# First attention: the key tiles that take a relative bias, moved to other places in the order of the scores

## The chip, the core and the metric

The program runs on one core of a Trainium2 chip. The metric is the device time of one execution in microseconds (us), as the median of several. TensorE is called PE here, VectorE DVE, ScalarE ACT, GpSimd POOL, and SP is the queue that issues most DMAs.

## What is computed

The input is 4096 tokens of 256 numbers. A first attention with 16 heads of 16 numbers, over all 4096 tokens, has a bias that depends on the clipped distance of query and key:

```
scores = jnp.einsum('bhid,bhjd->bhij', qh, kh)
rel = jnp.clip(pos[None, :] - pos[:, None], -K, K) + K          # K = 64
bias_r = jnp.einsum('bhid,rd->bhir', qh, rel_pe)
bias = jnp.take_along_axis(bias_r, jnp.broadcast_to(rel[None, None], (b, h, l, l)), axis=-1)
attn = jax.nn.softmax(scores + bias, axis=-1)
out = jnp.einsum('bhij,bhjd->bhid', attn, vh)
```

A layernorm and two layers of windowed attention and feed-forward follow. The change is in the first attention alone, which takes the span from about 250 to 3755 us.

## The kernel before

`attend` works through 128 chunks: 16 heads, each with 8 chunks of 512 queries. For a chunk all 32 tiles of 128 keys are scored. The keys are laid out so that tile 0 is the first of the chunk's own four tiles; tile 31 is the one just before them. Where query and key are more than 64 apart the bias is one of two edge values, which are part of the key rows, so the score matmul brings it along. Tiles 0, 1 and 2 need one edge on one side and the other on the other side: two matmuls (`score`, L516 and L519). Near the diagonal something has to be added: to tiles 0 to 4 and to tile 31, in all six additions of DVE (`near_add`, L741) from `near_bias` onto the scores in PSUM, 192, 256, 256, 192, 64 and 64 columns wide.

Scores come in **pairs** of tiles, 16 to a chunk (`PAIRS`). Pair s lies in the PSUM buffer `scores[s % 2]`; ACT makes its exponentials in one instruction (`exp_pair`, L642) into `probs`. `score` of pair s waits until the exponential of pair s - 2 is done. Where a pair takes additions, its exponential also waits for `near_added`.

Before a chunk can be scored its row maxima must be known. They come from 32 **max groups** (`max_group`, L490, with additions to the near ones by matmul, L494): each is one 512-wide matmul into one of three shared PSUM banks, which DVE reads with a reduce (`bank_max`, L765) before the bank is used again. These groups run 16 slots ahead of the chunk. The three banks are handed on in a fixed order (`SHARED_USES`), in which the two halves of a bias block (`make_bias`, L542, read by ACT in `keep_bias`, L633), the maxima turned to rows (L502) and the final sum of a chunk (L551) have places too: the bank of the first bias half is that of max group in slot 1, the next max groups take the banks after groups 2 and 3.

The order is written out by hand. A chunk has eight **turns** on PE; in each turn come the value matmuls of two pairs (`pv_quad`, L531), then four **slots**, each with one max group, and two pairs of scores behind the first and the second slot:

```
for turn in range(QUADS):
    pv_quad(n, par, turn)
    for i in range(4):
        slot = 4 * turn + i
        max_slot(n, par, bias, slot, ahead)
        for c in SLOT_SCORES[i]:        # ((0, 1), (2, 3), (), ())
            if turn < QUADS - 2:
                score(n, par, 4 * (turn + 2) + c)
            elif ahead:
                score(n + 1, 1 - par, 4 * (turn - QUADS + 2) + c)
```

So turns 0 to 5 score pairs 4 to 15 of the chunk, turns 6 and 7 pairs 0 to 3 of the next one. Turns 0 and 1 also hold the two halves of a bias block, in all chunks but the last nine. After turn 7 comes `sum_quadrants`, four transposes of `out_copy`, which ACT copies behind the exponential of pair 1.

DVE goes slot by slot: the read of the slot's max group, `near_add` ahead of some of them (`NEAR_SLOTS`), and at the end of the chunk `finish` (L773, L775, L777: out_sum, inv_sum, tokens). SP loads the keys for two chunks ahead in four pieces, each when a given pair has been scored (`PIECES`, third number). Chunks run two to a pass of a hardware loop on each engine.

Of the kernel before, what the change touches and what calls it, by code (L numbers as in the profile page):

```python
# [22 lines left out]
P = 128  # L23
# [3 lines left out]
TILES = N // P  # L27
# [7 lines left out]
CH = 512  # L35
CHUNKS = N // CH
TPC = CH // P
# [8 lines left out]
VW = D + 1  # L46
WIN_TILES = TILES + TPC - 1
SLAB = 2 * P
PAD = CLIP
PAIRS = TILES // 2  # L50
# [183 lines left out]
def attend(nc, q_parts, k_parts, v_wide, rel_T, ident, attn):  # L234
# [9 lines left out]
    LEAD = 16  # L244
    TOTAL = HEADS * CHUNKS
    SLOT_SCORES = ((0, 1), (2, 3), (), ())
    NEAR_SLOTS = (26, 27, 30, 23)
    ROWS_SLOT = 20
    MAX_GROUPS = TPC * (TILES // TPC)
    with ExitStack() as ctx:  # L250
# [3 lines left out]
        keys = [sb(f"keys{i}", [ROWS + MROWS, WIN_TILES * P], BF16) for i in range(2)]  # L254
        queries = [sb(f"queries{i}", [ROWS + MROWS, CH], BF16) for i in range(2)]
        max_queries = [sb(f"max_queries{i}", [ROWS, CH], BF16) for i in range(2)]
        values = [sb(f"values{i}", [P, TILES, VW]) for i in range(2)]
# [26 lines left out]
        out_ps = ps("out_ps", [P, CH])  # L284
# [11 lines left out]
        table_ready = sem("table_ready")  # L296
        cleared = sem("cleared")
        ident_ready = sem("ident_ready")
        PIECES = ((0, 8, 3), (8, 16, 7), (16, 24, 11), (24, WIN_TILES, 15))
        keys_in = [[sem(f"keys_in{i}_{j}") for j in range(4)] for i in range(2)]  # L300
        queries_in = [sem(f"queries_in{i}") for i in range(2)]
        max_queries_in = [sem(f"max_queries_in{i}") for i in range(2)]
# [13 lines left out]
        near_added = sem("near_added")  # L316
# [9 lines left out]
        def place(n):  # L326

            return n // CHUNKS, n % CHUNKS

        @block.sync  # L330
        def _(sp):
# [3 lines left out]
            def load_keys(n, par, j):  # L335
                h, c = place(n)
                a, b, _ = PIECES[j]
                row = 0
# [39 lines left out]
            with sp.Fori(0, TOTAL // 2 - 1) as m:  # L378
                for par in range(2):
# [3 lines left out]
                    for j in range(4):  # L383
                        sp.wait_ge(scores_ready, n * PAIRS + PIECES[j][2] + 1)
                        load_keys(n + 2, par, j)
# [74 lines left out]
        def _(pe):  # L460
# [45 lines left out]
            def score(n, par, c):  # L506

                s = c // 2
                if c == 0:
                    pe.wait_ge(queries_in[par], (n // 2) * QUERY_DMAS + QUERY_DMAS)  # L510
                    pe.wait_ge(max_placed, n + 1)
                if c % 2 == 0:
                    pe.wait_ge(exp_done, n * PAIRS + s + 1)
                cut = min(c + 1, TPC) * P
                out = scores[s % 2][:, c % 2, :]
                mm = pe.matmul(out[:, 0:cut], keys[par][:, c * P:(c + 1) * P],  # L516
                               queries[par][:, 0:cut], start=True, stop=True)
                if cut < CH:
                    mm = pe.matmul(out[:, cut:CH], keys[par][:, (c + TILES) * P:(c + TILES + 1) * P],  # L519
                                   queries[par][:, cut:CH], start=True, stop=True)  # L520
                if c % 2 == 1:
                    mm.then_inc(scores_ready, 1)

            def pv_quad(n, par, q):

                if q == 0:
                    pe.wait_ge(values_in[par], (n // 2) * 16 + 16)
                    pe.wait_ge(out_copied, n + 1)
                pe.wait_ge(exp_done, n * PAIRS + 2 * q + 4)
                for i in range(4):  # L530
                    mm = pe.matmul(out_ps[32 * i:32 * i + VW, :], values[par][:, 4 * q + i, :],  # L531
                                   probs[(2 * q + i // 2) % 4][:, i % 2, :],
                                   start=q == 0, stop=q == QUADS - 1, skip_group_check=True)
                mm.then_inc(pv_done, 1)
# [74 lines left out]
            for c in range(8):  # L609
                score(0, 0, c)  # L610
# [12 lines left out]
        @block.scalar  # L623
        def _(act):
            act.preload_act_table(ACT.Exp)
            act.sem_inc(exp_done, 2)
            for semaphore in (out_copied, normed, out_summed, max_rows):
                act.sem_inc(semaphore, 1)

            def keep_bias(block_no, half):  # L630
                h, b = place(block_no)
                act.wait_ge(bias_ready, block_no * 2 + half + 1)
                act.activation(near_bias[:, bass.ds(h % 2, 1), 1:TILES + 1, bass.ds(b * BLOCK_U + half * UG, UG)],  # L633
                               shared("bias", half).rearrange("p (a u j) -> p a j u", a=1, u=UG), ACT.Copy
                               ).then_inc(bias_read, 1)

            def exp_pair(n, s):
                if s in (0, 1, 2, PAIRS - 1):
                    act.wait_ge(near_added, n * 4 + {0: 1, 1: 2, 2: 3, PAIRS - 1: 4}[s])
                act.wait_ge(scores_ready, n * PAIRS + s + 1)  # L640
                act.wait_ge(pv_done, n * QUADS + s // 2 + 1)
                act.activation(probs[s % 4][:], scores[s % 2][:], ACT.Exp).then_inc(exp_done, 1)  # L642

            def place_max(n, par):
                act.wait_ge(max_rows, n + 2)
                act.activation(queries[par][ROWS:ROWS + MROWS, :], shared("rows", 0)[ROWS:ROWS + MROWS, :], ACT.Copy
                               ).then_inc(max_placed, 1)

            def chunk(n, par, bias, more):

                for s in range(4, PAIRS):
                    if s == PAIRS - 2 and more:
                        place_max(n + 1, 1 - par)
                    exp_pair(n, s)
                    if bias and s in (5, 7):
                        if s == 5:
                            act.wait_ge(window_ready, n + 1)
                        keep_bias(n + NEXT_GEN, s // 7)
                for s in range(4):
                    if more:  # L660
                        exp_pair(n + 1, s)
                    if s == 1:
                        act.wait_ge(pv_done, n * QUADS + QUADS + 2)
                        act.wait_ge(out_summed, n + 1)
                        act.activation(out_copy[:], out_ps[:], ACT.Copy).then_inc(out_copied, 1)

            act.wait_ge(cleared, 10)
            for e in range(NEXT_GEN):
                for half in range(2):
                    keep_bias(e, half)  # L670
            place_max(0, 0)
            for s in range(4):
                exp_pair(0, s)
            last_bias = (TOTAL - NEXT_GEN) // 2
            with act.Fori(0, last_bias) as m:
                for par in range(2):
                    chunk(m * 2 + par, par, True, True)
            chunk(2 * last_bias, 0, True, True)
            chunk(2 * last_bias + 1, 1, False, True)
            with act.Fori(last_bias + 1, TOTAL // 2 - 1) as m:  # L680
                for par in range(2):
                    chunk(m * 2 + par, par, False, True)
            chunk(TOTAL - 2, 0, False, True)
            chunk(TOTAL - 1, 1, False, False)

        @block.vector
        def _(dve):
# [43 lines left out]
            def near_add(n, s):  # L731
                h, c = place(n)

                spans = {0: [(0, 0, 192, 1, 64), (1, 64, 320, 2, 0)],
                         1: [(0, 192, 448, 3, 0), (1, 320, 512, 4, 0)],
                         2: [(0, 448, 512, 5, 0)],
                         PAIRS - 1: [(1, 0, 64, 0, 192)]}[s]
                dve.wait_ge(scores_ready, n * PAIRS + s + 1)
                for tile, a, b, slab, u in spans:
                    part = scores[s % 2][:, tile, a:b]  # L740
                    ins = dve.tensor_tensor(part, part,  # L741
                                            near_bias[:, bass.ds(h % 2, 1), bass.ds(c * TPC + slab, 1), u:u + b - a],
                                            ALU.add)
                ins.then_inc(near_added, 1)
# [35 lines left out]
            def chunk(n, par, ahead):  # L780
                for slot in range(MAX_GROUPS):
                    k = LEAD + slot
                    if slot == NEAR_SLOTS[3]:
                        near_add(n, PAIRS - 1)
                    if ahead and slot in NEAR_SLOTS[:3]:
                        near_add(n + 1, NEAR_SLOTS.index(slot))
                    if k < MAX_GROUPS and ahead >= 1:
                        bank_max(n + 1, 1 - par, k, shared("max", slot))
                    if k >= MAX_GROUPS and ahead >= 2:
                        bank_max(n + 2, par, k - MAX_GROUPS, shared("max", slot))  # L790
                    if ahead >= 1 and MAX_GROUPS - 1 <= k <= MAX_GROUPS + 1:
                        (find_max, cut_high, cut_low)[k - MAX_GROUPS + 1](n + 1, 1 - par)
                finish(n)
# [5 lines left out]
            cut_low(0, 0)  # L799
            for k in range(LEAD):  # L800
                bank_max(1, 1, k, shared_ps[(MAX_GROUPS + k) % 3][:])
            for s in range(3):
                near_add(0, s)
            with dve.Fori(0, TOTAL // 2 - 1) as m:
                for par in range(2):
# [1031 lines left out]
```

## Time and profile before

| | |
|---|---|
| median of 3 runs | 5559.55 us (5557.49 to 5559.81) |
| profiled execution | 5559.1 us, its span 5557.4 us |
| PE busy | 5118.3 us (92%) |
| DVE busy | 4185.6 us (75%) |
| ACT busy | 3111.0 us (56%) |
| max-group reads, L765 | 4096 of 686 ns |
| exponentials, L642 | 2048 of 1021 ns |
| additions, L741 | 768 of 334 ns on average |

The shares are averages over the whole program; the stage of the change has its own. Matmuls overlap in the records, so the gap between two starts says more than a duration, and the same holds for DVE: one instruction's record begins before the one ahead has ended.

### The profile page before, as it was taken

The numbers are of one execution on the slowest core, as the hardware profiler recorded it, in microseconds if no ns is written. First come the engines' busy times: TensorE is split into PE (matmuls) and PEld (weight loads), VectorE is DVE, ScalarE is ACT, GpSimd is POOL, SyncE is SP. The second block draws the span as 40 slices with busy tenths as digits, with TensorE's granted clock in tenths as the row PEclk, the third lists the DMA queues.
The fourth block names the chain that finished last, engine by engine and source line by source line (L and its number), as shares of the span: only waits on it lengthen the run. The fifth ranks groups of instructions, "written<-read, shape, count | busy, mean of one in ns | idle before, by whom it ended". The sixth has DMA issues, their size and how long they took to land. (4 is left out here: it accounts for less than half of the span.)

```text
span 5557.4 us, 114988 instructions
## 1 busy us (share of the span) xinstructions
PE 5118.3 (92%) x33760; PEld 2655.6 (48%) x33760; DVE 4185.6 (75%) x8817; ACT 3111.0 (56%) x4539; POOL 997.1 (18%) x791
## 2 busy tenths in 40 slices
PE   7599999999999999999999999998599989899989
PEld 4233333333333333333333333334488867788866
DVE  6488888888888888888888888871477744677755
ACT  4266666666666666666666666670266532456521
POOL 0211111111111111111111111100233310233211
PEclk9599999999999999999999999995699999999999
DMA  6312212212122122121221211211200000000010
GB/s 203 76 49 55 54 48 54 52 52 54 49 55 54 48 54 54 49 54 48 54 54 48 55 48 48 52 40 33 95 1 0 0 17 0 17 0 0 1 38 23
DMA packets 199610, 248.32 MB, mean 45 GB/s; under 512 B 60575, under 2 KB 128485, under 8 KB 197733
## 3 DMA queue, kind: packets, MB, share of 16 engines
q1 hardware_dynamic: 194388, 226.76, 14.9%
q0 software_dynamic: 5136, 20.45, 1.9%
q8 instruction: 50, 0.82, 0.1%
q14 instruction: 36, 0.29, 0.0%
HBM read 210.72 MB, written 36.18 MB: 44 GB/s over the span
## 5 line engine op out<-in xcount | busy, mean ns | idle before, releaser
L765 DVE TENSOR_REDUCE group_max<-shared_ps 128x1 f32<-128x512 f32 x4096 | 2668.6, 686 | 536.6 <-PE shared_ps L490 430.6
L642 ACT ACTIVATE probs<-scores 128x1024 f32<-128x1024 f32 x2048 | 2012.0, 1021 | 995.7 <-PE scores L516 619.4
L490 PE MATMUL shared_ps<-keys,max_queries 96*128 96x512 bf16 x4096 | 1444.0, 385 | 10.8 <-issue 1.7
L516 PE MATMUL scores<-queries,keys 98*128 98x512 bf16 (+3 forms) x4096 | 1212.8, 370 | 92.6 <-ACT probs L642 91.5
L531 PE MATMUL out_ps<-probs,values 128*17 128x512 f32 x8192 | 1079.1, 599 | 0.4 <-ACT probs L642 0.4
L490 PEld LDWEIGHTS shared_ps<-keys,max_queries 96*128 96x128 bf16 x4096 | 395.2, 96 | 1149.2 <-DVE group_max L765 544.2
L231 POOL TENSOR_TENSOR near_window<-near_bias,one_f 128x1536 bf16<-128x1536 f32 x128 | 351.4, 2746 | 2909.1 <-DVE max_parts L759 2263.7
L516 PEld LDWEIGHTS scores<-queries,keys 98*128 98x128 bf16 x4096 | 359.0, 98 | 466.2 <-ACT probs L642 242.8
L542 PE MATMUL shared_ps<-block_q,block_table 96*128 96x32 bf16 x4096 | 271.6, 233 | 107.6 <-POOL block_q L427 80.7
L542 PEld LDWEIGHTS shared_ps<-block_q,block_table 96*128 96x128 bf16 x4096 | 231.3, 114 | 197.9 <-issue 148.6
L1191 POOL TENSOR_TENSOR norm<-norm,layer_expo 128x16 f32<-128x16 f32 x64 | 186.2, 2910 | 705.4 <-DVE norm L1577 705.4
L1449 ACT ACTIVATE sim_prob<-sim_prob,shift,norm 128x256 f32<-128x256 f32 x512 | 299.5, 588 | 10.0 <-DVE shift L1647 10.0
L531 PEld LDWEIGHTS out_ps<-probs,values 128*17 128x17 f32 x8192 | 136.1, 95 | 264.7 <-issue 191.4
L494 PE MATMUL shared_ps<-ident_b,near_window 128*128 128x128 bf16 x1536 | 255.4, 220 | 0.0
L633 ACT ACTIVATE near_bias<-shared_ps 128x512 f32 (+1 forms) x256 | 152.8, 597 | 179.5 <-PE shared_ps L542 179.4
L741 DVE TENSOR_TENSOR scores<-scores,near_bias 128x192 f32<-128x192 f32 (+2 forms) x768 | 234.2, 334 | 20.7 <-PE scores L516 16.5
L1297 PEld LDWEIGHTS bank<-v_kept,prob_T 128*128 128x128 f32 x2048 | 238.2, 192 | 7.5 <-issue 2.0
L1297 PE MATMUL bank<-v_kept,prob_T 128*128 128x64 f32 x2048 | 235.8, 274 | 1.2 <-DVE tokens L1609 1.2
L1429 ACT ACTIVATE squares<-bank 128x512 f32<-128x512 f32 x128 | 76.5, 598 | 262.5 <-PE bank L1250 262.5
L494 PEld LDWEIGHTS shared_ps<-ident_b,near_window 128*128 128x128 bf16 x1536 | 151.3, 99 | 123.3 <-issue 2.2
L1504 ACT ACTIVATE gate<-quad,b 128x512 f32<-128x512 f32 x96 | 66.1, 688 | 236.9 <-PE quad L1371 236.9
L1642 DVE CUSTOM_DVE_ANT_0 sim_prob<-quad,mask 128x256 f32<-128x256 f32 x512 | 181.9, 420 | 16.5 <-issue 13.3
(195 smaller groups left out, 5777.3 us busy)
## 6 DMA issues: line engine op xcount, KB each, us to landing
keys<-k_parts SPq DMA_DIRECT2D x384, 96.0 KB, 2.1
values<-v_wide SPq DMA_DIRECT2D x128, 272.0 KB, 2.7
keys<-k_parts SPq DMA_DIRECT2D x384, 64.0 KB, 2.0
keys<-k_parts SPq DMA_DIRECT2D x128, 132.0 KB, 2.4
k_parts<-part SPq DMA_DIRECT2D x96, 128.0 KB
queries<-q_parts SPq DMA_DIRECT2D x768, 16.0 KB, 1.7
max_queries<-q_parts SPq DMA_DIRECT2D x768, 16.0 KB, 1.7
keys<-k_parts SPq DMA_DIRECT2D x384, 32.0 KB, 1.9
```

Of the source, the lines that this page charges most:

```text
L231: return pool.tensor_tensor(out, in_, ones[:].to_broadcast(list(in_.shape)), ALU.mult)
L490: mm = pe.matmul(bank, max_queries[par][:, t * P:(t + 1) * P], keys[par][0:ROWS, (t + TPC * g) * P:(t + TPC * (g + 1)) * P], start=True, s ...
L494: mm = pe.matmul(bank[:, pos * P:(pos + 1) * P], near_window[par][:, slab, u:u + P], ident_b[:], start=False, stop=i == len(near) - 1)
L516: mm = pe.matmul(out[:, 0:cut], keys[par][:, c * P:(c + 1) * P], queries[par][:, 0:cut], start=True, stop=True)
L531: mm = pe.matmul(out_ps[32 * i:32 * i + VW, :], values[par][:, 4 * q + i, :], probs[(2 * q + i // 2) % 4][:, i % 2, :], start=q == 0, stop ...
L542: mm = pe.matmul(shared("bias", half)[:, i * TILES:(i + 1) * TILES], block_table[par][:, BLOCK_U - 1 - u:BLOCK_U - 1 - u + P], block_q[par ...
L642: act.activation(probs[s % 4][:], scores[s % 2][:], ACT.Exp).then_inc(exp_done, 1)
L741: ins = dve.tensor_tensor(part, part, near_bias[:, bass.ds(h % 2, 1), bass.ds(c * TPC + slab, 1), u:u + b - a], ALU.add)
L765: dve.tensor_reduce(group_max[par][:, k:k + 1], bank, AX.X, ALU.max).then_inc(max_read, 1)
L1191: pool.tensor_tensor(norm[par][:], norm[par][:], expo[:, 0:2 * LHEADS].rearrange("p (h a) -> p h a", a=1), ALU.pow).then_inc(S.norm_ready, 1)
L1297: mm = pe.matmul(o_ps[:, j * LD:(j + 1) * LD], prob_T[:, 2 * j + c, :], v[:, h * LD:(h + 1) * LD], start=c == 0, stop=c == 1)
L1449: ins = act.activation(prob[:, h, :], sim[:, h, :], ACT.Exp, bias=shift[:, head:head + 1], scale=norm[par][:, head, :], accum_out=total[:, ...
```

## The change

The order of the key tiles becomes a table, `ORDER`: place c of a chunk's 32 scores holds tile `ORDER[c]`. The same table selects the values in `pv_quad`. Tiles with additions are now in pair 2 (tile 0), 3 (tile 1), 4 (tile 2), 5 (tiles 3 and 4) and 10 (tile 31); before they were in pair 0 (tiles 0 and 1), 1 (tiles 2 and 3), 2 (tile 4) and 15 (tile 31). DVE does them in front of other slots, and two key pieces are released by other pairs.

```diff
-    NEAR_SLOTS = (26, 27, 30, 23)
+    ORDER = (5, 6, 7, 8, 0, 9, 1, 10, 2, 11, 3, 4, 12, 13, 14, 15, 16, 17, 18, 19, 20, 31,
+             21, 22, 23, 24, 25, 26, 27, 28, 29, 30)
+    NEAR_SPANS = {2: [(0, 0, 192, 1, 64)], 3: [(0, 64, 320, 2, 0)], 4: [(0, 192, 448, 3, 0)],
+                  5: [(0, 320, 512, 4, 0), (1, 448, 512, 5, 0)], 10: [(1, 0, 64, 0, 192)]}
+    NEAR_PAIRS = tuple(NEAR_SPANS)
+    NEAR_SLOTS = {30: 2, 31: 3, 2: 4, 3: 5, 14: 10}
...
-        PIECES = ((0, 8, 3), (8, 16, 7), (16, 24, 11), (24, WIN_TILES, 15))
+        PIECES = ((0, 8, 5), (8, 16, 7), (16, 24, 12), (24, WIN_TILES, 15))
...
-                cut = min(c + 1, TPC) * P
+                tile = ORDER[c]
+                cut = min(tile + 1, TPC) * P
...
-                    mm = pe.matmul(out_ps[32 * i:32 * i + VW, :], values[par][:, 4 * q + i, :],
+                    mm = pe.matmul(out_ps[32 * i:32 * i + VW, :], values[par][:, ORDER[4 * q + i], :],
...
-                if s in (0, 1, 2, PAIRS - 1):
-                    act.wait_ge(near_added, n * 4 + {0: 1, 1: 2, 2: 3, PAIRS - 1: 4}[s])
+                if s in NEAR_PAIRS:
+                    act.wait_ge(near_added, n * len(NEAR_PAIRS) + NEAR_PAIRS.index(s) + 1)
...
-                spans = {0: [(0, 0, 192, 1, 64), (1, 64, 320, 2, 0)],
-                         1: [(0, 192, 448, 3, 0), (1, 320, 512, 4, 0)],
-                         2: [(0, 448, 512, 5, 0)],
-                         PAIRS - 1: [(1, 0, 64, 0, 192)]}[s]
...
-                    if slot == NEAR_SLOTS[3]:
-                        near_add(n, PAIRS - 1)
-                    if ahead and slot in NEAR_SLOTS[:3]:
-                        near_add(n + 1, NEAR_SLOTS.index(slot))
+                    if slot in NEAR_SLOTS:
+                        if NEAR_SLOTS[slot] >= 4:
+                            near_add(n, NEAR_SLOTS[slot])
+                        elif ahead:
+                            near_add(n + 1, NEAR_SLOTS[slot])
...
-            for s in range(3):
+            for s in NEAR_PAIRS[:2]:
                 near_add(0, s)
```

Lines behind the table stand eight or fewer lines later in the new file: the reads of max groups are L769 there, the additions L745.

DVE in turns 6 and 7, before (`group_max` is the read of one max group, slot 26 the first shown; rows that set registers are left out):

```order
L741 TENSOR_TENSOR scores0<-scores0,near_bias 128x192
L741 TENSOR_TENSOR scores0<-scores0,near_bias 128x256
L765 TENSOR_REDUCE group_max0<-shared_ps2 128x1
...
L741 TENSOR_TENSOR scores1<-scores1,near_bias 128x256
L741 TENSOR_TENSOR scores1<-scores1,near_bias 128x192
L765 TENSOR_REDUCE group_max0<-shared_ps0 128x1
...
L741 TENSOR_TENSOR scores0<-scores0,near_bias 128x64
...
L773 TENSOR_REDUCE out_sum<-shared_ps2 128x68
```

DVE from slot 29 in turn 7 to the end of the chunk, after:

```order
L769 TENSOR_REDUCE group_max0<-shared_ps2 128x1
...
L745 TENSOR_TENSOR scores0<-scores0,near_bias 128x192
...
L769 TENSOR_REDUCE group_max0<-shared_ps0 128x1
...
L745 TENSOR_TENSOR scores1<-scores1,near_bias 128x256
...
L769 TENSOR_REDUCE group_max0<-shared_ps1 128x1
L777 TENSOR_REDUCE out_sum<-shared_ps2 128x68
...
L781 TENSOR_TENSOR tokens<-out_sum,inv_sum 128x4x16
```

Pairs 0 and 1 had two additions each ahead of slots 26 and 27; now slots 28 and 29 are read first, and one addition each stands ahead of slots 30 and 31, just before the end of the chunk.

DVE in turn 0, from slot 1 to slot 3, after (before, the four reads of this turn stood there with nothing between them):

```order
L769 TENSOR_REDUCE group_max0<-shared_ps1 128x1
...
L745 TENSOR_TENSOR scores0<-scores0,near_bias 128x256
...
L769 TENSOR_REDUCE group_max0<-shared_ps2 128x1
...
L745 TENSOR_TENSOR scores1<-scores1,near_bias 128x192
...
L745 TENSOR_TENSOR scores1<-scores1,near_bias 128x64
...
L769 TENSOR_REDUCE group_max0<-shared_ps0 128x1
```

The additions on pairs 4 and 5 have moved between the reads of slots 1, 2 and 3.

## Rows read from the trace of the kernel before

**Rows 1.** Busy time in a stretch of the steady stage: PE, weight loads, DVE, ACT, POOL, granted clock, DMA share, GB/s.

```profile
1000.00:1600.00 600.00, 578.15 (x3992) 220.02 (x3991) 503.17 (x956) 392.30 (x437) 97.10 (x82) 1.00 0.21 52
```

**Rows 2.** Waits from 400 to 3400 us: us in total, times, longest.

```profile
PEld scores L516 <- ACT probs L642: 198.7, 327, 0.9
...
ACT probs L642 <- DVE scores L741: 314.5, 370, 1.7
```

**Rows 3.** Timeline of PE, a turn without waits: start, us, instruction.

```profile
2002.44 1.05 PE L531 MATMUL out_ps<-probs,values 128*17 128x512 f32 x8
...
2003.43 0.39 PE L490 MATMUL shared_ps<-keys,max_queries 96*128 96x512 bf16 x1
...
2003.65 0.60 PE L516 MATMUL scores<-queries,keys 98*128 98x512 bf16 x2
...
2005.27 1.05 PE L531 MATMUL out_ps<-probs,values 128*17 128x512 f32 x8
```

**Rows 4.** Timeline of PE, turns 6 to 1, second kind of chunk.

```profile
2016.31 0.38 PE L490 MATMUL shared_ps<-keys,max_queries 96*128 96x512 bf16 x1
2016.63 0.34 PE L516 MATMUL scores<-queries,keys 98*128 98x384 bf16 x1
...
2017.60 1.05 PE L531 MATMUL out_ps<-probs,values 128*17 128x512 f32 x8
2018.58 0.39 PE L490 MATMUL shared_ps<-keys,max_queries 96*128 96x512 bf16 x1
...
2019.33 0.61 PE L516 MATMUL scores<-queries,keys 98*128 98x512 bf16 x2 [0.35 <-ACT probs L642]
2019.77 0.38 PE L490 MATMUL shared_ps<-keys,max_queries 96*128 96x512 bf16 x1
2020.56 0.61 PE L516 MATMUL scores<-queries,keys 98*128 98x512 bf16 x2 [0.41 <-ACT probs L642]
...
2025.46 1.07 PE L542 MATMUL shared_ps<-block_q,block_table 96*128 96x32 bf16 x16 [0.28 <-DVE group_max L765]
```

**Rows 5.** Timeline of DVE: additions, reads, the end of two chunks (first and second kind).

```profile
1995.22 0.43 DVE L773 TENSOR_REDUCE out_sum<-shared_ps 128x68 f32<-128x272 f32 x1
...
1996.22 2.47 DVE L765 TENSOR_REDUCE group_max<-shared_ps 128x1 f32<-128x512 f32 x4
...
2015.16 0.22 DVE L741 TENSOR_TENSOR scores<-scores,near_bias 128x64 f32<-128x64 f32 x1
...
2017.34 0.71 DVE L741 TENSOR_TENSOR scores<-scores,near_bias 128x192 f32<-128x192 f32 x2
2017.96 0.68 DVE L765 TENSOR_REDUCE group_max<-shared_ps 128x1 f32<-128x512 f32 x1
2018.56 0.69 DVE L741 TENSOR_TENSOR scores<-scores,near_bias 128x256 f32<-128x256 f32 x2
...
2022.62 0.43 DVE L773 TENSOR_REDUCE out_sum<-shared_ps 128x68 f32<-128x272 f32 x1
...
2024.04 2.48 DVE L765 TENSOR_REDUCE group_max<-shared_ps 128x1 f32<-128x512 f32 x4 [0.33 <-PE shared_ps L490]
```

**Rows 6.** Timeline of ACT, the exponential of pair 0.

```profile
2018.25 1.02 ACT L642 ACTIVATE probs<-scores 128x1024 f32<-128x1024 f32 x1 [1.68 <-DVE scores L741]
```

**Rows 7.** Timeline of PE, turn 7 and the bias half, first kind.

```profile
1990.29 1.05 PE L531 MATMUL out_ps<-probs,values 128*17 128x512 f32 x8
...
1997.63 1.07 PE L542 MATMUL shared_ps<-block_q,block_table 96*128 96x32 bf16 x16 [0.17 <-DVE group_max L765]
```

**Rows 8.** Timeline of PE, end of chunk, two chunks apart: with a bias block, and without.

```profile
1994.03 0.60 PE L551 MATMUL shared_ps<-ident_f,out_copy 128*128 128x128 f32 x4
...
2049.16 0.60 PE L551 MATMUL shared_ps<-ident_f,out_copy 128*128 128x128 f32 x4
...
3613.05 0.60 PE L551 MATMUL shared_ps<-ident_f,out_copy 128*128 128x128 f32 x4
...
3663.53 0.60 PE L551 MATMUL shared_ps<-ident_f,out_copy 128*128 128x128 f32 x4
```

More of the change, by code:

```diff
@@ L513, in score @@
                     pe.wait_ge(exp_done, n * PAIRS + s + 1)
-                cut = min(c + 1, TPC) * P
+                tile = ORDER[c]
+                cut = min(tile + 1, TPC) * P
                 out = scores[s % 2][:, c % 2, :]
-                mm = pe.matmul(out[:, 0:cut], keys[par][:, c * P:(c + 1) * P],
+                mm = pe.matmul(out[:, 0:cut], keys[par][:, tile * P:(tile + 1) * P],
                                queries[par][:, 0:cut], start=True, stop=True)
                 if cut < CH:
-                    mm = pe.matmul(out[:, cut:CH], keys[par][:, (c + TILES) * P:(c + TILES + 1) * P],
+                    mm = pe.matmul(out[:, cut:CH], keys[par][:, (tile + TILES) * P:(tile + TILES + 1) * P],
                                    queries[par][:, cut:CH], start=True, stop=True)
@@ L732, in near_add @@
                 h, c = place(n)
-                spans = {0: [(0, 0, 192, 1, 64), (1, 64, 320, 2, 0)],
-                         1: [(0, 192, 448, 3, 0), (1, 320, 512, 4, 0)],
-                         2: [(0, 448, 512, 5, 0)],
-                         PAIRS - 1: [(1, 0, 64, 0, 192)]}[s]
                 dve.wait_ge(scores_ready, n * PAIRS + s + 1)
-                for tile, a, b, slab, u in spans:
+                for tile, a, b, slab, u in NEAR_SPANS[s]:
                     part = scores[s % 2][:, tile, a:b]
```

## Prediction, made before the change was run

> **What bounds the kernel now.** I read the stretches of the first attention first. In its steady stage PE is busy 578 of 600 us, DVE 503 and ACT 392, at a granted clock of 1.00 (2.4 GHz) [rows 1]; nothing in DMA comes near. So PE carries the time, and the question is where it stands still. The Trainium skill (Perfetto Trace Analysis, Identifying the Most-Contended Engine) says that matmul busy time is no measure of TensorE's headroom, since pipelined matmuls overlap in it. The trace agrees: a wait that the timeline books as 0.35 us idle is longer when it is measured from start to start (below).
>
> The list of waits over 3000 us, 109 chunks, comes next: ACT waited 314.5 us for DVE's additions to the scores, and the weight loads of the scores waited 198.7 us for ACT's exponentials [rows 2]. The chain is addition (DVE), exponential (ACT), next scores into the same buffer (PE).
>
> Then the timeline of one chunk. A turn without trouble starts its next turn 2.83 us later; its first max group starts 0.99 us after the value matmuls, the scores 0.22 us behind that group [rows 3]. In turn 6 and 7 it looks different [rows 4]: pair 1 starts 0.32 us behind its group instead of 0.22; pair 2 starts 0.75 us behind group 28 (0.53 lost), pair 3 0.79 us behind group 29 (0.57 lost). Pair 0 had been scored by about 2016.5, but its exponential started at 2018.25 after 1.68 us idle [rows 6], because DVE reaches its two additions only at 2017.34 [rows 5] and both stand in front of it. So 1.20 us per chunk go to the additions on pairs 15, 0 and 1.
>
> Who would be late next? After turn 7 PE goes through the sum and turn 0 to the first half of the bias block. Its bank is that of max group 1, which DVE must have read, behind the end of the chunk (out_sum, inv_sum, tokens). From the start of turn 7 to the bias matmuls it takes 7.34 us in one kind of chunk [rows 7] and 7.86 in the other [rows 4]. The two kinds alternate: DVE needs 1.00 us from out_sum to the next read, and 1.42 us where its loop turns round [rows 5]. Already here the bias matmuls start right as DVE ends its second read: in the second kind 2024.04 + 0.60 + 0.69 = 2025.33, bias at 2025.46. **The DVE chain is thus the limit of the stretch already, with the ACT waits in front of it.**
>
> **The change, part by part.** No matmul, read, addition or exponential is added or removed; the six additions keep their widths. A wait per chunk on ACT is added (five marked pairs, not four), one DVE wait on scores too, both on semaphores that are long up.
>
> *Pairs 0 and 1 lose their additions.* Their exponentials then start when scored: pair 0 in turn 6 from about 2016.5 to 2017.5, pair 1 to 2018.5; pairs 2 and 3 are wanted at 2018.8 and 2019.5. Both waits (0.53 and 0.57 us) go. Pair 15 loses its 64-wide addition (0.22 us [rows 5]), and with it the 0.10 us at pair 1 in turn 6.
>
> *What DVE does then in turn 7.* Measured from the value matmuls of turn 7. Group 28 starts at 0.99 and has landed at 1.4. From there DVE has four reads, 0.60 us from one to the next (2017.96 to 2018.56), and the additions on pairs 2 (192 wide) and 3 (256 wide). Those two widths together took 0.62 us in pair 0 (2017.34 to 2017.96) [rows 5]. With 0.05 us of waiting for group 29, out_sum starts at 1.4 + 2.40 + 0.62 + 0.05 = 4.5. Then 1.00 (1.42) us, the two reads of 0.60 + 0.69, and 0.12 us to PE: the bias block starts at **6.9 (7.3)** where it started at 7.34 (7.86). Gain 0.43 (0.53) us. The rest of the 1.10 us is given back, as PE waits for DVE in turn 0. With the 0.10 of turn 6 it is 0.53 (0.63).
>
> *Turn 0.* DVE now has three additions more there: pair 4 (256 wide) before the read of group 2, pair 5 (192 and 64) before group 3, about 0.74 us. They stand behind the read that the bias waits for. The block (1.0 us of PE [rows 4]) hides them. DVE's first read of the turn starts at 4.5 + 1.0 = 5.5; with three steps of 0.60, the 0.74 us of additions and 0.69 us for the last read, group 3 is read by 8.7 (9.1 in the other kind). PE's value matmuls of turn 1 start at 6.9 + 1.0 = 7.9, group 4 0.99 us later, group 5, which wants that bank, another 0.65 us later: 9.5 (9.9). The exponentials follow: pair 4 from 7.3 (its addition ends at 7.1, and ACT follows some 0.2 us later) to 8.3, pair 5 to 9.3; PE wants them for pair 6 at 9.1 and pair 7 at 9.75. ACT's copy of the first bias half then ends at 9.9, and group 6 wants the bank at 10.2. All are hidden by 0.2 us or more, but only by the bias block. For the exponentials of pairs 2 and 3, wanted by pairs 4 and 5 at 4.6 and 5.25, I get 4.2 and 5.2: the tightest place.
>
> *Chunks without a bias block* (the last nine). That cover is missing. DVE ends group 2 at 7.7, where group 4 wants the bank, and group 3 at 8.7, where group 5 wants it at 8.5. They lose some 0.3 us there and gain about as much before: no change. Two of them take 50.5 us now [rows 8].
>
> *Pair 10.* Its 64-wide addition in turn 3 delays the exponentials of pairs 10 and 11 by some 0.2 us each; pair 13, which needs the latter, is wanted in turn 4 at 2.1 us from its start, when it is just done. I cost it at nothing; above, 0.1 us, as pair 15 cost before.
>
> *DMA.* Key piece 0 is released after pair 5 and not pair 3, some 2 us later, piece 2 after pair 12 and not 11. SP has the queries of the max groups to issue in between, and piece 0 is first needed in turn 4, some 10 us on. Nothing.
>
> *Score matmuls.* Tiles 0 to 2 keep their two parts; they are done in turns 7 and 0. Their columns are the same in number. Nothing.
>
> **Sum.** Two neighbouring chunks gain 0.53 + 0.63 = 1.16 us; 119 chunks have a bias block, so 59.5 x 1.16 = 69 us. The profiled execution took 5559.1 us (span 5557.4), the median of the runs is 5559.55. 5559.1 - 69 = **5490 us**.
>
> Bounds per chunk: at the most 1.20 us, everything that the additions cost now; at the least, the gain less what the tight places could cost, 0.1 at pair 13 and 0.15 at pairs 4 and 5: 0.33 us. I stay near the DVE chain, since it is made of measured steps.
>
> **Rivals.**
>
> *A. All waits go, DVE keeps up* (0.15). Then 1.20 us x 127 = 152 us, 5407 us. For it: DVE is idle 16% of the stage [rows 1]. Against: the idle time lies in other turns, and by the chain above DVE ends later than PE in turn 7. The Trainium skill (same page and section) holds that for VectorE occupancy is a fair measure of how close an engine is to its limit. By that rule DVE at 84% would leave room, and this rival would be right.
>
> *B. The tight places cost* (0.17). ACT starts each of the exponentials of pairs 2 to 5 a little later than I count, pairs 4, 5 and 13 wait: 0.33 us, 119 x 0.33 = 39 us, 5520 us.
>
> *C. Slower* (0.07). DVE carries turn 0's additions into turn 1: PE waits for the bank of group 3, and all 0.74 us of them come on its path while 0.58 are gained. That is +0.16 us x 119 = 19 us, 5578 us. It decides from the point where DVE's read of group 3 ends after 9.5, 0.8 us later than I have it. The chunks without a bias block show this mechanism in small.
>
> *D. Nothing moves* (0.05). The bias block starts when it did, because the stretch from out_sum on is held by something that the profile doesn't show: 5559 us. Against: both kinds of chunk fit the DVE chain, with 0.12 and 0.13 us between its last read and the bias matmuls.
>
> **How the numbers follow.** My forecast has 0.56. About 0.2% (11 us) is what a measurement of this kernel can tell from no change. Forecast, A and B are faster: 0.88; D same: 0.05; C slower: 0.07. The range goes from 5430, nearly three quarters of the way to A, to 5545, beyond B.
>
> **What would show it.** The period of two chunks falls from 55.1 to about 54.0 us. ACT's waits for additions shrink in turns 6 and 7 and reappear in turns 7 and 0; pairs 2 and 3 start 0.22 us behind their groups. The bias matmuls of turn 0 still wait for DVE, now longer, and start 6.9 or 7.3 us after turn 7. If turn 7 to bias takes under 6.5 us, A holds; if group 5 waits for a read in turn 1, C; if pairs 4, 5 or 13 wait for an exponential, B. I am wrong altogether if turns 2 to 5 have changed length.

## The result, and the profile after

The changed kernel takes 5522.61 us (median of 4 runs, 5516.73 to 5526.94); the kernel before took 5559.68 us in the 4 runs beside it. The ratio is 0.9932, with a 95% interval from 0.9915 to 0.9949: faster by 0.7%. I had forecast 5490 us, in a range from 5430 to 5545. The direction was right, and about half of the forecast gain came.

The change shows in the stage of the attention. Timeline of PE, end of a chunk, two chunks apart with a bias block, then two apart without (as [rows 8]):

```profile
2027.10 0.66 PE L559 MATMUL shared_ps<-ident_f,out_copy 128*128 128x128 f32 x4
...
2081.07 0.66 PE L559 MATMUL shared_ps<-ident_f,out_copy 128*128 128x128 f32 x4
...
3574.82 0.66 PE L559 MATMUL shared_ps<-ident_f,out_copy 128*128 128x128 f32 x4
...
3625.98 0.66 PE L559 MATMUL shared_ps<-ident_f,out_copy 128*128 128x128 f32 x4
```

Two chunks take 53.97 us, where they took 55.13; 54.0 was forecast. The chunks without a bias block have got slower, 51.16 us for two against 50.48.

Timeline of PE in turn 7 and turn 0, first kind of chunk, and the bias block of the second kind (as [rows 4] and [rows 7]):

```profile
2024.29 1.05 PE L539 MATMUL out_ps<-probs,values 128*17 128x512 f32 x8
2025.28 0.39 PE L497 MATMUL shared_ps<-keys,max_queries 96*128 96x512 bf16 x1
2025.50 0.22 PE L524 MATMUL scores<-queries,keys 98*128 98x128 bf16 x1
...
2027.69 1.05 PE L539 MATMUL out_ps<-probs,values 128*17 128x512 f32 x8
...
2031.17 1.07 PE L550 MATMUL shared_ps<-block_q,block_table 96*128 96x32 bf16 x16 [0.28 <-DVE group_max L769]
```

```profile
1997.10 1.05 PE L539 MATMUL out_ps<-probs,values 128*17 128x512 f32 x8
...
2000.67 1.05 PE L539 MATMUL out_ps<-probs,values 128*17 128x512 f32 x8
...
2003.72 0.39 PE L497 MATMUL shared_ps<-keys,max_queries 96*128 96x512 bf16 x1 [0.37 <-DVE group_max L769]
2004.39 1.07 PE L550 MATMUL shared_ps<-block_q,block_table 96*128 96x32 bf16 x16 [0.28 <-DVE group_max L769]
```

Pair 2 starts 0.22 us behind group 28. From turn 7 to the bias block it is 2031.17 - 2024.29 = 6.88 us and 2004.39 - 1997.10 = 7.29 us; 6.9 and 7.3 were forecast. PE's wait has moved from turn 7, on ACT, into turn 0, on DVE.

DVE over the same stretch (as [rows 5]), from the addition on pair 2 to the read of group 3:

```profile
1999.77 0.35 DVE L745 TENSOR_TENSOR scores<-scores,near_bias 128x192 f32<-128x192 f32 x1
2000.04 0.68 DVE L769 TENSOR_REDUCE group_max<-shared_ps 128x1 f32<-128x512 f32 x1
2000.63 0.42 DVE L745 TENSOR_TENSOR scores<-scores,near_bias 128x256 f32<-128x256 f32 x1
2000.96 0.68 DVE L769 TENSOR_REDUCE group_max<-shared_ps 128x1 f32<-128x512 f32 x1
2001.56 0.43 DVE L777 TENSOR_REDUCE out_sum<-shared_ps 128x68 f32<-128x272 f32 x1
...
2002.97 1.29 DVE L769 TENSOR_REDUCE group_max<-shared_ps 128x1 f32<-128x512 f32 x2 [0.33 <-PE shared_ps L497]
2004.18 0.42 DVE L745 TENSOR_TENSOR scores<-scores,near_bias 128x256 f32<-128x256 f32 x1
2004.51 0.68 DVE L769 TENSOR_REDUCE group_max<-shared_ps 128x1 f32<-128x512 f32 x1
2005.11 0.49 DVE L745 TENSOR_TENSOR scores<-scores,near_bias 128x192 f32<-128x192 f32 x2
2005.50 0.68 DVE L769 TENSOR_REDUCE group_max<-shared_ps 128x1 f32<-128x512 f32 x1
```

out_sum starts 1997.10 + 4.46, against 4.5 in the forecast; the second read after it is the one that lets the bias block go.

**So where are the other 33 us?** Of the 128 chunks, 19 take 28.7 or 28.8 us from one end to the next, all of the second kind, whose others take 27.2. In the kernel before none stands out. One of them, in stretches of 1 us (the columns are those of [rows 1]); its bias block starts at 966.18:

```profile
965.70:966.70 1.00, 0.72 (x11) 0.53 (x11) 1.00 (x3) 0.12 (x1) 0.00 (x0) 1.00 0.41 100
966.70:967.70 1.00, 1.00 (x14) 0.50 (x15) 1.00 (x4) 1.00 (x2) 0.00 (x0) 0.90 0.29 96
967.70:968.70 1.00, 1.00 (x8) 0.00 (x0) 0.26 (x1) 1.00 (x2) 0.00 (x0) 0.50 0.00 0
968.70:969.70 1.00, 1.00 (x7) 0.40 (x4) 0.30 (x1) 0.36 (x1) 0.00 (x0) 0.50 0.00 0
969.70:970.70 1.00, 1.00 (x4) 0.34 (x3) 0.41 (x2) 0.37 (x1) 0.00 (x0) 0.50 0.00 0
970.70:971.70 1.00, 1.00 (x7) 0.48 (x6) 0.84 (x2) 1.00 (x2) 0.00 (x0) 0.89 0.00 0
971.70:972.70 1.00, 1.00 (x21) 0.88 (x22) 1.00 (x2) 0.64 (x1) 0.00 (x0) 1.00 0.15 29
```

The granted clock falls from 1.00 (2.4 GHz) to 0.50 (1.2 GHz) just after the bias block, and comes back some 3.4 us later. All 19 falls of the stage begin at this place, 5.4 to 5.9 us after the transposes that end a chunk. Before it fell, PE had waited 0.40 and 0.28 us for DVE and then done the block's 32-column matmuls. Each fall costs 1.6 us: 19 x 1.6 = 30 us. The rest of the account: from the first chunk's end to that of chunk 118 it is 3214.4 us, where it was 3253.0, so 38.6 less (68.4 of periods, less 30 of falls); the nine chunk ends after it take 3.8 us more (217.9 for 214.2); 0.5 and 0.9 us are gained before and after. That is the 36.2 us by which the span is shorter (5521.2 for 5557.4).

### The profile page after: what moved, and what is told of

It reads as the page before. It is cut to its first block and busy times, and to the rows that moved or that the text cites. A ratio compares the mean times of both kernels' runs of the same rounds, so it can differ in the third digit from the quotient of the medians.

```text
span 5521.2 us, 115238 instructions
## 1 busy us (share of the span) xinstructions
PE 5134.7 (93%) x33760; PEld 2668.6 (48%) x33760; DVE 4184.3 (76%) x8817; ACT 3086.9 (56%) x4539; POOL 997.2 (18%) x791
## 5 line engine op out<-in xcount | busy, mean ns | idle before, releaser
L769 DVE TENSOR_REDUCE group_max<-shared_ps 128x1 f32<-128x512 f32 x4096 | 2690.6, 686 | 500.5 <-PE shared_ps L497 405.9
L650 ACT ACTIVATE probs<-scores 128x1024 f32<-128x1024 f32 x2048 | 1987.1, 1021 | 1070.2 <-DVE scores L745 760.4
L497 PE MATMUL shared_ps<-keys,max_queries 96*128 96x512 bf16 x4096 | 1463.7, 387 | 35.9 <-DVE group_max L769 26.2
L524 PE MATMUL scores<-queries,keys 98*128 98x512 bf16 (+3 forms) x4096 | 1236.3, 373 | 4.6 <-ACT probs L650 2.7
L539 PE MATMUL out_ps<-probs,values 128*17 128x512 f32 x8192 | 1092.6, 605 | 5.5 <-ACT probs L650 0.6
L524 PEld LDWEIGHTS scores<-queries,keys 98*128 98x128 bf16 x4096 | 374.1, 99 | 305.8 <-ACT probs L650 38.4
L745 DVE TENSOR_TENSOR scores<-scores,near_bias 128x192 f32<-128x192 f32 (+2 forms) x768 | 244.1, 333 | 18.3 <-PE scores L524 18.1
```

Of the source, the lines that this page charges most:

```text
L497: mm = pe.matmul(bank, max_queries[par][:, t * P:(t + 1) * P], keys[par][0:ROWS, (t + TPC * g) * P:(t + TPC * (g + 1)) * P], start=True, s ...
L524: mm = pe.matmul(out[:, 0:cut], keys[par][:, tile * P:(tile + 1) * P], queries[par][:, 0:cut], start=True, stop=True)
L745: ins = dve.tensor_tensor(part, part, near_bias[:, bass.ds(h % 2, 1), bass.ds(c * TPC + slab, 1), u:u + b - a], ALU.add)
L769: dve.tensor_reduce(group_max[par][:, k:k + 1], bank, AX.X, ALU.max).then_inc(max_read, 1)
```

## Experiments

The kernel before was timed again beside them: 5560.48 us beside experiments 1, 2 and 6, and 5561.33 us beside 3, 4 and 5. Each ratio is to that time.

**1. Filling the wait.** In turn 0, the max-group matmuls of slots 2 and 3 are repeated, into the same bank, before DVE is told:

```diff
+                for _ in range({LEAD + 2: 3, LEAD + 3: 2}.get(k, 1)):
-                mm = pe.matmul(bank, max_queries[par][:, t * P:(t + 1) * P],
+                    mm = pe.matmul(bank, max_queries[par][:, t * P:(t + 1) * P],
...
```

> The changed kernel, with the max-group matmuls of slots 2 and 3 in turn 0 done three times and twice (the same result into the same bank, before DVE is told), so that PE works where it waited for DVE. In the trace of the changed kernel the period of two chunks is 53.97 us, as forecast, but some 19 single chunks take 1.6 us longer, and in them the granted clock is 0.50 for about 3.6 us from the bias block of turn 0 on. Theory W: the clock falls because PE does little in that place (0.65 us of waits in one piece and narrow bias matmuls). Then the falls go, the period stays 53.97, the three extra matmuls (0.65 us) are hidden in the waits, and the time is 5522.6 - 30 = 5492 us. Rival P: the clock falls because the chip works harder as a whole; then more matmuls keep or add falls: 5522 us or more. Rival N: the added matmuls aren't hidden: 127 x 0.65 = 83 us more at the most.

It took 5495.97 us (5495.09 to 5496.41), ratio 0.9885 (0.9869 to 0.9902). The periods are 26.77 and 27.2 us as before, in all 118 intervals up to the last bias block, with none of 28.8. The stretch of [rows 1] in this kernel, and below it in the changed one:

```profile
1000.00:1600.00 600.00, 598.43 (x4140) 231.41 (x4139) 514.91 (x980) 395.51 (x445) 101.16 (x85) 1.00 0.21 53
```

```profile
1000.00:1600.00 600.00, 587.27 (x4030) 224.50 (x4026) 509.44 (x968) 391.68 (x441) 99.50 (x84) 0.99 0.20 53
```

More work for PE at the same period makes the program 27 us faster. Rivals P and N fall: it is the thin place in turn 0 that lets the clock fall, and not the load as a whole. The experiment fills the wait and leaves the narrow matmuls of the bias block. These alone don't make the clock fall, since the kernel before has them too and stays at 1.00; whether the wait would do it without them is not shown. The added matmuls are useless work; they only show the cause.

**2. A second read on DVE, at the end of turn 7.** In the changed kernel and in the one before, the bank of slot 31 is read twice:

```diff
+                if k == LEAD - 1:
+                    dve.tensor_reduce(spare[:], bank, AX.X, ALU.max)
                 dve.tensor_reduce(group_max[par][:, k:k + 1], bank, AX.X, ALU.max
...
```

> The changed kernel, in which DVE reads the bank of slot 31 twice (the first time into a spare column): 0.60 us more per chunk on DVE just before the end of the chunk. Theory: the DVE chain from turn 7 to the bias block sets the period, so all of it comes out: 127 x 0.60 = 76 us, 5599 us, and with longer waits of PE in one place more falls of the clock on top (each 1.6 us; up to one per chunk, 190 us). Rival: DVE has room (it is idle 15% of the stage), and under 20 us come out.

> The kernel before, with the same second read of the bank of slot 31. Theory of the prediction: already before, the DVE chain was the limit of the stretch and the ACT waits stood in front of it; then 0.60 us per chunk come out, 76 us, 5636 us (more with falls of the clock). Rival: before, PE was held by ACT's exponentials alone and DVE had slack at slot 31; then the second read is hidden, under 20 us.

The changed kernel took 5656.38 us (ratio to the kernel before 1.0168, 1.0151 to 1.0185), the one before 5734.84 us (1.0313, 1.0296 to 1.033). The undisturbed periods grew from 26.77 and 27.2 to 27.37 and 27.79: 0.60 us each, all of it. In the kernel before they grew from 27.40 and 27.72 to 28.04 and 28.32, by 0.64 and 0.60. Two neighbouring chunks without a fall, by the transposes at their ends, in the changed kernel and then in the one before:

```profile
793.22 0.66 PE L560 MATMUL shared_ps<-ident_f,out_copy 128*128 128x128 f32 x4
...
820.60 0.66 PE L560 MATMUL shared_ps<-ident_f,out_copy 128*128 128x128 f32 x4
...
848.39 0.66 PE L560 MATMUL shared_ps<-ident_f,out_copy 128*128 128x128 f32 x4
```

```profile
1303.50 0.60 PE L552 MATMUL shared_ps<-ident_f,out_copy 128*128 128x128 f32 x4
...
1331.82 0.60 PE L552 MATMUL shared_ps<-ident_f,out_copy 128*128 128x128 f32 x4
...
1359.86 0.60 PE L552 MATMUL shared_ps<-ident_f,out_copy 128*128 128x128 f32 x4
```

So the DVE chain from slot 31 on set the period in both kernels, though without the second read DVE is busy for only 84% (before) and 85% (changed) of the stage. The rest of the loss is falls of the clock. In the changed kernel 35 chunks took 28.9 us or more: 23 of the second kind and 12 of the first. Eleven of the 35 took 32.1, and in these the clock was down for 10.2 us. In the kernel before 54 took 29.7 or more, all of the second kind, which has 59. Above the undisturbed periods these chunks come to 85 us in the changed kernel and 97 in the one before.

**3. The same with the wait filled**, both changes together in each kernel.

> The changed kernel with the second read at slot 31 and, in slots 2 and 3 of turn 0, the same repeated max-group matmuls as in the first experiment. Without them the second read cost 134 us, of which 0.60 us a chunk are the DVE chain (periods of 27.37 and 27.79 us, against 26.77 and 27.19). Theory: the rest is the clock's falls, which the filled wait removes: 5496 + 76 = 5572 us with no chunk above 27.8 us. Rival: the falls have another cause and stay: 5650 us.

> The kernel before with the second read at slot 31 and the repeated max-group matmuls in turn 0. Without them the second read cost 174 us, and nearly every chunk after the loop's turn took 29.9 us. Theory: 0.60 to 0.65 us a chunk are the DVE chain, the rest the falls: 5560 + 80 = 5640 us. Rival: another price of the second read in this kernel, 5700 us or more.

5576.85 us (5572.12 to 5580.25) and 5642.13 us (5640.78 to 5642.69). The first still has four chunks of 29.4 us, where none above 27.8 had been expected; the second has none above 28.5. Against the filled kernel of experiment 1, the second read costs 80.9 us. The four falls are 6.5 of them, which leaves 0.59 a chunk. Against the kernel before it costs 81 us, 0.64 a chunk. The filled kernels are 80 and 93 us faster than the unfilled ones: with the second read, the clock took as much as the read itself, or more.

**4. Tile 31 alone.** The kernel before, with tile 31 in pair 10 and its addition at slot 14. Key piece 2 is also released by pair 12 and not 11, as in the changed kernel:

```diff
-    NEAR_SLOTS = (26, 27, 30, 23)
+    NEAR_SLOTS = (26, 27, 30, 14)
+    ORDER = tuple(range(21)) + (31,) + tuple(range(21, 31))
...
```

> The kernel before with one part of the change alone: tile 31 goes from pair 15 to pair 10 and its addition from slot 23 to slot 14. By the prediction pair 1 in turn 6 no longer waits 0.10 us for the exponential of pair 15, and pair 13 in turn 4 loses nothing. Behind turn 6 stand the additions on pairs 0 and 1 and the DVE chain, and DVE has 0.13 us less to do before them: 0.10 us x 127 = 13 us less, 5547 us. Rival: DVE reaches the additions on pair 0 at the same time as before (it waits for group 25), so nothing comes out at the end of turn 7, and the time is 5560 us.

5567.93 us (11 runs) against 5561.33: ratio 1.0012 (1.0003 to 1.0021). A little slower, where 13 us of gain had been expected. Its PE timeline, from the start of turn 4 into turn 7, and its additions on pair 0; below them, the starts of turns 4, 5 and 6 in the kernel before:

```profile
2013.97 1.05 PE L534 MATMUL out_ps<-probs,values 128*17 128x512 f32 x8
...
2017.30 1.05 PE L534 MATMUL out_ps<-probs,values 128*17 128x512 f32 x8
...
2020.34 1.05 PE L534 MATMUL out_ps<-probs,values 128*17 128x512 f32 x8
...
2023.17 1.05 PE L534 MATMUL out_ps<-probs,values 128*17 128x512 f32 x8
...
2025.02 0.60 PE L519 MATMUL scores<-queries,keys 98*128 98x512 bf16 x2 [0.47 <-ACT probs L645]
```

```profile
2023.02 0.72 DVE L744 TENSOR_TENSOR scores<-scores,near_bias 128x192 f32<-128x192 f32 x2
```

```profile
2008.33 1.05 PE L531 MATMUL out_ps<-probs,values 128*17 128x512 f32 x8
...
2011.61 1.05 PE L531 MATMUL out_ps<-probs,values 128*17 128x512 f32 x8
...
2014.66 1.05 PE L531 MATMUL out_ps<-probs,values 128*17 128x512 f32 x8
```

Turn 6 takes 2.83 us and not 2.94, as said. But the additions on pair 0 start 2.68 us after turn 6 in both kernels (2017.34 - 2014.66 before, 2023.02 - 2020.34 here), so the wait of pair 2 grows by the same 0.1 us (0.47 idle for 0.35). And turn 4 takes 3.33 us where it took 3.28: pair 13 does wait for the exponential of pair 11. Each period is 0.05 us longer, x 127 = 7 us. The rival was right that nothing comes out at the end of turn 7, and the price that I had put at nothing is 0.05 us a chunk.

**5. A second read in turn 0**, in the changed kernel, at slot 3 (`if k == LEAD + 3`), behind the reads for the bias block.

> The changed kernel with a second read of 0.60 us at slot 3 of turn 0 and not at slot 31: behind the read that the bias block waits for, and behind the additions on pairs 4 and 5. By the prediction this place has 0.8 us of room before PE wants the bank for group 5 (the point from which rival C decides), and the bias block covers it: only the nine chunks without one pay, 5 us, 5528 us. If the room isn't there, what comes out is up to 76 us, 5599 us.

5525.56 us (5522.15 to 5532.04), with periods of 26.78 and 27.2 us, unchanged to 0.01, and 23 long chunks for 19. The chunks without a bias block pay, 25.60 and 26.01 us for 25.37 and 25.80, which is 2 us in all and not 5. The same 0.60 us of DVE costs 0.60 in turn 7, and four reads later it leaves the periods as they were: the bias block does cover turn 0.

**6. The additions later still.** The changed kernel with no addition in turn 7. Tiles 1 and 2 are in pair 4, 3 and 4 in pair 5, tile 0 in pair 6:

```diff
-    ORDER = (5, 6, 7, 8, 0, 9, 1, 10, 2, 11, 3, 4, 12, 13, 14, 15, 16, 17, 18, 19, 20, 31,
+    ORDER = (5, 6, 7, 8, 9, 10, 11, 12, 1, 2, 3, 4, 0, 13, 14, 15, 16, 17, 18, 19, 20, 31,
...
-    NEAR_SLOTS = {30: 2, 31: 3, 2: 4, 3: 5, 14: 10}
+    NEAR_SLOTS = {2: 4, 3: 5, 6: 6, 14: 10}
...
-        PIECES = ((0, 8, 5), (8, 16, 7), (16, 24, 12), (24, WIN_TILES, 15))
+        PIECES = ((0, 8, 6), (8, 16, 7), (16, 24, 12), (24, WIN_TILES, 15))
```

Tiles 1 to 4 must be added to by pair 5, since ACT writes the first columns of the next but one head's bias behind that exponential.

> The changed kernel with the marked tiles later still: tiles 1 and 2 in pair 4, 3 and 4 in pair 5, 0 in pair 6, 31 in pair 10. DVE has no addition in turn 7, and they stand behind the reads that the bias block waits for. Theory (DVE chain): turn 7 to bias falls from 6.9 (7.3) to 6.26 (6.7) us, 0.62 us x 119 = 74 us, 5448 us; with shorter waits the clock's falls may go too, 30 us more, 5418 us. Rival: the 0.94 us of additions in turn 0 come on PE's path through the exponentials of pairs 4 and 5 or the bank of group 3, and the gain is under 20 us, or it is slower.

5431.16 us (5430.65 to 5432.07), ratio 0.9769 (0.9752 to 0.9785): 91 us faster than the changed kernel, and the best of all. Its periods are 26.25 and 26.66 us, 0.53 and 0.54 less and not 0.62, and no chunk is long. Timeline of PE, turn 7 and the bias block, of both kinds:

```profile
2000.90 1.05 PE L539 MATMUL out_ps<-probs,values 128*17 128x512 f32 x8
...
2007.66 1.07 PE L550 MATMUL shared_ps<-block_q,block_table 96*128 96x32 bf16 x16 [0.28 <-DVE group_max L769]
...
2027.56 1.05 PE L539 MATMUL out_ps<-probs,values 128*17 128x512 f32 x8
...
2033.90 1.07 PE L550 MATMUL shared_ps<-block_q,block_table 96*128 96x32 bf16 x16
```

6.34 and 6.76 us, for 6.26 and 6.7 expected. Of the missing 0.09, most is in how DVE runs in turn 7:

```profile
2002.31 2.59 DVE L769 TENSOR_REDUCE group_max<-shared_ps 128x1 f32<-128x512 f32 x4 [0.23 <-PE shared_ps L497]
2004.82 0.43 DVE L777 TENSOR_REDUCE out_sum<-shared_ps 128x68 f32<-128x272 f32 x1
```

DVE takes 2.51 us from the first of these four reads to out_sum, where back to back it would be 2.40: it must be waiting for groups to land between its reads. No addition is left in this stretch, so that little should be left to gain there by placing; no run tries it. Of the 92 us by which the attention is shorter than in the changed kernel, 59 x 1.07 = 63 are periods and 30 the falls; the first and the last chunks take up to 1 us back.

## Why the prediction was right, and where not

**Right, by its own steps.** The waits of pairs 2 and 3 went. The DVE chain is the limit, before and after: out_sum at 4.46 (4.5 said), bias block at 6.88 and 7.29 (6.9 and 7.3), two chunks 53.97 (54.0), and experiment 2 shows it by itself: a read put on the chain comes out whole. Rival A, that DVE keeps up, is thereby out. Its 152 us were also too high: the 1.20 us of waits had been read from a chunk of the second kind, and in the first kind pairs 2 and 3 start 0.71 and 0.72 us behind their groups (1991.27 to 1991.98, 1992.43 to 1993.15), which makes 1.09. The Trainium skill (Perfetto Trace Analysis, Identifying the Most-Contended Engine) calls occupancy on VectorE a fair measure of how close one is to the roofline. It says nothing of room at a given place here: with DVE occupied for 84 to 85%, there was none at the end of turn 7 (experiment 2), and 0.60 us of it in turn 0 (experiment 5). Rival C's point of decision was right too: the room in turn 0 was there (experiment 5). Rival B's tight places at pairs 4 and 5 cost nothing; the one at pair 13 does (below).

**Mis-sized: the sum's step "119 chunks have a bias block, so 59.5 x 1.16".** It let every chunk run at the clock of [rows 1]. Nineteen didn't, which took 30 of the 69 us; this is why only about half of the forecast gain came, and the range was wide enough for it by luck, since nothing in it stood for the clock. That the time came near rival B's 5520 us is chance too: of its mechanism only pair 13's 0.05 us a chunk was there. I had written that the rest of the gain "is given back, as PE waits for DVE in turn 0", and saw in it a matter of length only. In fact the wait of a chunk was put into one place, next to the narrow matmuls of the bias block: 3.72 us from the value matmuls of turn 0 to the bias block in the second kind (2000.67 to 2004.39), against 3.48 in the first (2027.69 to 2031.17), where no chunk was long. In the kernel before it was 3.50 us in the second kind (2021.96 to 2025.46), with the rest of the idle time in turn 7, and the clock never fell there, so the rows before gave no warning. The Trainium skill does (TensorE: Matmul & The Clock Gate, "A second HAM failure mode: psum-queue depth-cycling"): short idle times between groups that cycle through PSUM banks can make the clock go back and forth. This case agrees, with 19 falls of 1.6 us; the prediction had no term for it.

**Wrong: "They lose some 0.3 us there and gain about as much before: no change"** for the chunks without a bias block. They lose 0.3 us net. I had followed the banks of groups 4 and 5, but not pair 6, which now waits for the exponential of pair 4:

```profile
3578.62 0.39 PE L497 MATMUL shared_ps<-keys,max_queries 96*128 96x512 bf16 x1 [0.40 <-DVE group_max L769]
...
3580.15 0.39 PE L497 MATMUL shared_ps<-keys,max_queries 96*128 96x512 bf16 x1 [0.15 <-DVE group_max L769]
3580.78 0.61 PE L524 MATMUL scores<-queries,keys 98*128 98x512 bf16 x2 [0.24 <-ACT probs L650]
```

It is 4 us in all, with the last chunks. **Wrong: "I cost it at nothing"** for pair 10; it is 0.05 us a chunk, some 6 us. The gain per two chunks is still 1.16 us as forecast, because the other parts gave a little more than their terms (0.46 and 0.57 us from turn 7 to the bias block, for 0.43 and 0.53), which makes up most of it. That the periods agree so closely is in part luck. And the 0.10 us of pair 15 is a gain only because the additions on pairs 0 and 1 go as well; alone it is worth nothing (experiment 4).

What stays open: why the falls hit some chunks and not their likes. They aren't scattered: in the changed kernel they follow each other after four and six chunks in turn, with one longer gap, and in the kernel before with a second read they come at nearly every chunk of the second kind. What sets this spacing is not shown. Filling the wait removes all falls in two kernels and leaves four in a third. Lengthening it adds some, but not in proportion: with the second read, 35 chunks are long in the changed kernel and 54 in the kernel before, though from the value matmuls of turn 0 to the bias block it is 4.35 us in the first and only 4.09 in the second.

## What to carry to other kernels

When one wait is removed, follow the next engine's chain to the wait that takes its place, step by step between starts; done so, it forecast the period of two chunks to 0.1%, with a little luck. Then look at the shape of what is left: idle time gathered in one place can cost again through TensorE's clock. Here that was 30 us in the changed kernel, and as much as the added read itself in experiment 2. Work for another engine belongs behind the instruction that TensorE waits for, under the longest stretch of TensorE's own work.

## What the hardware did that I had not expected

- A wait of about 0.9 us in turn 0 (3.72 us to the bias block, where it is 2.81 in turn 1, which has no waits: 2005.39 to 2008.20), with narrow matmuls behind it, cost 1.6 us more in 19 of 128 chunks, the granted clock being 0.50 (1.2 GHz) for some 3.4 us. Three repeated 512-column matmuls in that wait removed all of it.
- One more read of 0.60 us on DVE cost 134 and 174 us in 128 chunks, of which about 75 and 81 were the read (0.59 and 0.64 us a chunk).
- Once in two chunks, where DVE's loop turns, it is 1.42 us from out_sum to the next read and not 1.00. In the changed kernel these 0.4 us come out in full in every second chunk (27.2 us for 26.77). That they belong to the loop is inferred from their place: the trace books them as a wait for a max group that had long been done (it started at 2001.66, the read at 2002.97).
